# Experts of 64 in L2: slots of 32 rows in four column tiles instead of 64 rows in two, with sixteen weight homes

## The chip, the cores and the metric

The kernel runs on one core of a Trainium2 chip, in one launch. The metric is the device time of that launch in microseconds (us); lower is better. Before the change it is 2492.97 us, the median of three runs (2492.96 to 2495.43).

## The reference, cut to what matters

A chain of graph layers and mixture-of-experts layers over 625 nodes of 512 features. The change touches one of them, `L2_ffn`: each node picks 6 of 64 experts (a sigmoid router with a bias, first the best 4 of 8 groups of experts, then the best 6 in them), each picked expert computes a gated hidden layer of 160, and the six results are added with the node's weights. A shared expert of width 512 is added for all nodes.

```python
shared = jax.nn.silu(xf @ sWg) * (xf @ sWu) @ sWd
scores = jax.nn.sigmoid(xf @ router_w.T)
biased = scores + bias_corr
...
_, topk_idx = jax.lax.top_k(masked, 6)
w = jnp.take_along_axis(scores, topk_idx, axis=1)
w = w / (w.sum(axis=-1, keepdims=True) + 1e-20)
g = jnp.einsum('sc,ech->seh', xf, Wg)      # 512 -> 160, for each of 64 experts
u = jnp.einsum('sc,ech->seh', xf, Wu)
routed = jnp.einsum('seh,ehc->sc', combine[:, :, None] * jax.nn.silu(g) * u, Wd)
```

The kernel computes only the 3750 pairs of a node and a picked expert. A program that evaluates the reference on its inputs gives how they fall on the experts: 27 of the 64 get any rows, from 1 to 510 each, 3750 in all.

## The kernel before, in words

**Slots.** Rows of one expert are packed into slots of 64 rows; an expert with c rows takes ceil(c/64) slots. The worst case is 122 slots, so the program has 61 passes (`NU`) of two slots, one in each half of 128 rows. Every pass is in the program whether its slots have rows or not.

**Two blocks.** `l2_experts_block` (L2269) runs the router on DVE and the shared expert on PE side by side, then makes the tables: which expert owns each slot (`owner`, L2512), and which row sits in which place of which slot. The second table is built by 30 steps (L2524 to L2529): for each, DVE writes two one-hot operands (L2527 `place_hot`, L2529 `slot_value`), and PE multiplies them for each half (L2408), adding up in PSUM. PE then does the shared expert's `down` (L86 there). SyncE (SP) loads the first passes' weights (L2326 and on) and POOL gathers the first rows.

`l2_routed_blocks` (L2625) is the loop over passes. In iteration u of it, in this order, PE turns the rows of pass u+1 (`rows_transposed`, L2694), turns the hidden rows of pass u-1 (`hidden_transposed`, L2723; every fourth pass also the last 32 hidden columns of four passes at once, L2715), multiplies gate and up of pass u (`gate_up`, L2706: 4 k-tiles by 2 halves of 64 columns of the array, 320 columns streamed), multiplies the first 128 hidden columns of pass u-1 with Wd (`down`, L2731), and after every fourth pass the remaining 32 of four passes (`rest_down`, L2741). The two halves are column tiles of the array (`tile_position=(0, 64 * h)`): each has its own weights and rows. ACT copies the turned rows out (L2767) and computes silu (L2777). DVE multiplies (L2809, L2813), copies the turned hidden rows (L2790, L2796) and the result (L2803). POOL gathers rows eight passes ahead (L2557) and scatters results (L2563).

**Weights.** SP issues them by an order written out by hand. A pass u has for each half one main load (`Wgud`, 896 KB, L2597) and one rest load (64 KB, L2598). There are eight homes (`WR`) for mains, so pass u shares its homes with passes u-4, u-8 and so on; the slots are numbered so that such a chain holds neighbouring slots, mostly of one expert. A main is therefore fetched only when the expert changes within its home (`cond=new`), while a rest is fetched for every slot with rows (`cond=used`); a load that is left out is still issued, as an instruction that moves nothing. Expert numbers and conditions come from three tables, read eight entries at a time for four passes (L2591). The mains of pass u wait for `down(u-4)` (semaphore `d_mm`), which has read the same homes; rests wait for the `rest_down` two groups back (`y_mm`), as they have two buffers. The first two passes' weights are issued in the block ahead. At its start this block's SP also issues the next layer's weights (W1, W2 and three small ones, L2657 to L2661).

## Time and profile before

| | |
|---|---|
| median of 3 runs | 2492.97 us |
| the profiled execution | 2492.98 us, its span 2491.2 us |
| granted TensorE clock over the span | 0.964 of full |
| busy, share of the span | PE 94%, DVE 45%, ACT 29%, POOL 26% |
| moved by DMA | 281.58 MB, mean 113 GB/s |

The profile is of one execution. All windows are counted in us from the start of its span. The loop over passes runs from about 1834 to 2098 us, a tenth of the span. `PE` rows are matmuls, `PEld` rows are weight loads, `SPq` rows are instructions of SP's queue. An fp32 matmul of the program is two matmul instructions in the trace.

### The profile page before, as it was taken

How to read it: one execution, taken by the hardware profiler on the slowest of the kernel's cores; microseconds unless marked ns; L12 is line 12 of the kernel's file. 1: busy time of each engine (PE TensorE's matmuls, PEld its weight loads, DVE VectorE, ACT ScalarE, POOL GpSimd, SP SyncE). 2: the span in 40 equal slices, each digit the busy share in tenths (PEclk: the TensorE clock that was granted, in tenths of full speed). 3: DMA queues.
4: the chain of work that ended last, by engine and by line, in shares of the span. 5: the costliest groups of instructions: out<-in, count | busy, mean ns of one | idle time of the engine just before them, and what ended most of it. 6: DMA issues, size and time to landing. Idle time of an engine off the chain costs nothing. (4 is left out here: it accounts for less than half of the span.)

```text
span 2491.2 us, 33816 instructions
## 1 busy us (share of the span) xinstructions
PE 2335.4 (94%) x11401; PEld 1509.1 (61%) x11401; DVE 1126.0 (45%) x2712; ACT 717.6 (29%) x1398; POOL 649.4 (26%) x652
## 2 busy tenths in 40 slices
PE   5898969999999999999999999999989998889998
PEld 4475547757757765466576576576644444457775
DVE  8733985545545546735344344253623333530002
ACT  0422333323343322225134144153212221112211
POOL 0563666506506510000101101001124542101110
PEclk9898989999999998999999999999989998979999
DMA  3122026517507523020110110010056553558885
GB/s 90 49 72 72 1 84 213 147 31 232 150 28 228 152 69 112 17 81 1 58 60 22 37 60 23 34 51 13 18 174 230 176 187 116 123 201 306 319 292 194
DMA packets 73533, 281.58 MB, mean 113 GB/s; under 512 B 22298, under 2 KB 22426, under 8 KB 65438
## 3 DMA queue, kind: packets, MB, share of 16 engines
q1 hardware_dynamic: 38363, 188.09, 22.1%
q0 software_dynamic: 35008, 91.33, 12.4%
q8 instruction: 102, 1.67, 0.3%
q14 instruction: 60, 0.49, 0.1%
HBM read 354.71 MB, written 30.43 MB: 155 GB/s over the span
## 5 line engine op out<-in xcount | busy, mean ns | idle before, releaser
L86 PE MATMUL ps<-XT,W 128*128 128x250 f32 (+1 forms) x1200 | 334.6, 434 | 3.5 <-ACT XT L1420 1.6
L86 PEld LDWEIGHTS ps<-XT,W 128*128 128x128 f32 x1200 | 228.5, 193 | 106.1 <-issue 21.7
L1150 PE MATMUL ps<-XN,W 128*128 128x512 f32 x498 | 256.7, 598 | 2.6 <-ACT GT L1472 2.6
L1856 POOL TENSOR_TENSOR H<-H,RB 125x512 f32<-125x512 f32 x40 | 50.6, 1267 | 724.0 <-DVE XN L2179 611.6
L2706 PE MATMUL ps<-W,HT 128*64 128x320 f32 x976 | 146.2, 442 | 4.7 <-issue 4.7
L2563 POOL DMA_INDIRECT result_rows<-KT,LOGC x77 | 78.3, 1017 | 260.5 <-DVE KT L3292 212.7
L86 PE MATMUL ps<-W,HT 128*128 128x512 f32 (+1 forms) x312 | 139.9, 602 | 0.8 <-ACT HT L3261 0.5
L86 PEld LDWEIGHTS ps<-HT,W 128*128 128x128 f32 x1088 | 126.5, 195 | 8.8 <-issue 7.7
L86 PE MATMUL ps<-HT,W 128*128 128x128 f32 x1088 | 126.7, 278 | 0.8 <-DVE HT L3272 0.8
L1126 POOL DMA_INDIRECT XT<-node_rows,LOGC x81 | 77.1, 952 | 173.8 <-DMA node_rows<-V 122.3
L1288 PEld LDWEIGHTS ps<-P,QT 128*128 128x128 f32 x672 | 89.2, 194 | 44.4 <-issue 44.4
L1288 PEld LDWEIGHTS ps<-P,KT 128*128 128x128 f32 x672 | 88.1, 192 | 39.7 <-issue 39.7
L3261 ACT ACTIVATE HT<-ps,lcols 128x128 f32<-128x128 f32 x136 | 50.1, 368 | 211.3 <-PE ps L86 211.3
L1288 PEld LDWEIGHTS ps<-P,XT 128*128 128x128 f32 x648 | 85.2, 193 | 41.6 <-issue 41.4
L2232 DVE CUSTOM_DVE_ANT_0 P<-ps,LOGC 125x626 f32<-125x626 f32 x80 | 64.6, 807 | 96.0 <-PE ps L94 96.0
L86 PE MATMUL ps<-HT,V 125*128 125x125 f32 x800 | 102.7, 275 | 0.0
L2706 PEld LDWEIGHTS ps<-W,HT 128*64 128x64 f32 x976 | 65.4, 138 | 61.5 <-issue 16.1
L86 PEld LDWEIGHTS ps<-W,HT 128*128 128x128 f32 (+1 forms) x312 | 58.2, 191 | 71.7 <-issue 66.8
L94 PE MATMUL ps<-KT,QT 128*125 128x313 f32 x320 | 98.8, 430 | 0.0
L1126 POOL DMA_INDIRECT QT<-node_rows,LOGC x84 | 79.8, 950 | 65.4 <-PE ps L1288 42.7
L86 PEld LDWEIGHTS ps<-HT,V 125*128 125x128 f32 x800 | 95.7, 192 | 0.3
L1126 POOL DMA_INDIRECT KT<-node_rows,LOGC x84 | 79.4, 946 | 56.0 <-PE ps L1288 44.5
(618 smaller groups left out, 4175.4 us busy)
## 6 DMA issues: line engine op xcount, KB each, us to landing
W<-in_L_ffn_Wgud SPq DMA_DIRECT2D x122, 896.0 KB
W<-in_L_ffn_w SPq DMA_DIRECT2D x36, 2048.0 KB, 7.8
W<-in_L_gnn_Wqkv SPq DMA_DIRECT2D x4, 3072.0 KB, 9.9
W<-in_L_gnn_W SPq DMA_DIRECT2D x5, 2048.0 KB, 14.9
W<-in_L_gnn_Wm SPq DMA_DIRECT2D x4, 2048.0 KB, 7.7
W<-in_L_ffn_Wd_rest SPq DMA_DIRECT2D x122, 64.0 KB
W<-result_rows SPq DMA_DIRECT2D x5, 1344.0 KB
RB<-in_L_gnn_rows SPq DMA_DIRECT2D x24, 256.0 KB, 4.2
```

Source lines behind the costliest of these rows:

```text
L86: last = nc.tensor.matmul(out, lhs(k), rhs(k), start=(k == 0), stop=(k == nk - 1))
L94: last = nc.tensor.matmul(slot[0:m, a, 0:HF], lhs(k), rhs(k)[:, a * HF:(a + 1) * HF], start=(k == 0), stop=(k == nk - 1))
L1126: nc.gpsimd.indirect_dma_start(edges[n % GR], None, hb, bass.IndirectOffsetOnAxis(ap=b.slot_src[:, t:t + 1], axis=0)).then_inc(arrived[n % ...
L1150: nc.tensor.matmul(b.ps[:, n % PR, :], b.EAT[:, t * 128:(t + 1) * 128], We[layer], start=True, stop=True)\
L1288: last = nc.tensor.matmul(sums[:, k * 128:][:, bass.ds(off, R)], edges[n % GR][:, k * 128:(k + 1) * 128], hot[n % HR], start=False, stop=F ...
L1856: ins = nc.gpsimd.tensor_tensor(b.H[0:R, t, :], b.H[0:R, t, :], b.RB[0:R, at:at + D], ALU.add)
L2232: v.tensor_tensor_reduce(out=halves(P[i % 5]), in0=b.slot(0)[0:R, :, 0:HF], in1=halves(b.LOGC[0:R, t, :]), scale=1.0, scalar=-3e38, op0=AL ...
L2563: self.nc.gpsimd.indirect_dma_start(self.rows, bass.IndirectOffsetOnAxis(ap=self.b.slot_row[:, sl:sl + 1], axis=0), out, None, bounds_chec ...
L2706: last = nc.tensor.matmul(b.ps[HALF[h], 1 + u % 2, 0:2 * HE], xT[u % 2][:, k, HALF[h]], Wgu[(2 * u + h) % WR][:, k, :], start=(k == 0), st ...
L3261: nc.scalar.activation(hT[u][:, m, :], b.ps[:, 1 + m % 4, 0:128], ACT.Relu, bias=r.bias[u][:, m:m + 1]).then_inc(s["hidden_ready"], 1)
```

## The change

Slots have 32 rows, an expert with c rows takes ceil(c/32) of them, and a pass holds four, in the four column tiles of 32. The worst case is 180 slots, so there are 45 passes for 61. Four passes of four mains have sixteen homes, which lie in parts of eight tensors (`W`, `H`, `XN`, `V`, `P`, `XT`, `LOGC`, `HT`). Pass u still shares its homes with u-4. A rest load has one buffer for each home now, is fetched only when its main is (`step[4 + j]` conditions both), waits for the `rest_down` of the group before, and is issued two passes behind its main. There is one table, read for every pass (`read_step`). The next layer's W1 and W2 lie where homes are, so they are issued at the end of the loop. Rows are gathered six passes ahead for eight. In the block ahead the tables are 180 columns wide for 122, and the 30 steps multiply four quarters of 32.

The core of the diff (the index expressions of the tables that only change width are left out):

```diff
-    NE, NG, TG, K, NU, NH = r.ne, 8, 4, r.k, r.ns, 2 * r.ns
+    NE, NG, TG, K, NU, NH = r.ne, 8, 4, r.k, r.ns, 4 * r.ns
...
-            experts, news, useds = r.read_steps(sp, 0, 2 * r.early)
+            r.step_registers = [[sp.alloc_register(f"step{i}_{j}") for j in range(8)] for i in range(r.WR)]
             for u in range(r.early):
-                for h in range(2):
-                    r.load_weights(sp, u, h, experts[2 * u + h], news[2 * u + h], useds[2 * u + h])
+                step = r.read_step(sp, u)
+                for j in range(4):
+                    if u == 1 and j == 2:
+                        sp.wait_ge(s["up_mm"], len(units))
+                    r.load_main(sp, u, j, step)
...
-            for x in (*r.in_rows[0:4], vf[:, 375:384], vf[:, 634:2048]):
+            for x in (*r.in_rows[0:4], r.in_rows[5], vf[:, 2048:2560]):
...
-            pool.wait_ge(s["cleared"], 6)
+            nc.gpsimd.memset(r.in_rows[4], 0.0).then_inc(s["cleared"], 1)
+            pool.wait_ge(s["cleared"], 7)
...
-                for h in range(2):
-                    last = nc.tensor.matmul(b.ps[64 * h:64 * h + 64, 7, 0:NU], place_hot[j % RING],
+                for h in range(4):
+                    last = nc.tensor.matmul(b.ps[32 * h:32 * h + 32, 7, 0:NU], place_hot[j % RING],
                                             slot_value[j % RING][:, NU * h:NU * (h + 1)], start=(j == 0),
-                                            stop=(j == T * K - 1), tile_position=(0, 64 * h))
+                                            stop=(j == T * K - 1), tile_position=(0, 32 * h))
                 last.then_inc(s["table_mm"], 1)
...
-                v.tensor_scalar(place_hot[j % RING], b.iota[0:R, 0:64], in_slot[:, j:j + 1], None, ALU.is_equal)\
+                v.tensor_scalar(place_hot[j % RING], b.iota[0:R, 0:32], in_slot[:, j:j + 1], None, ALU.is_equal)\
...
-    WR, RR, GR, GU, early = 8, 2, 8, KD * 320, 2
-    CHAINS = WR // 2
+    WR, GR, GU, early = 4, 6, KD * 320, 2
 
     def __init__(self, nc, b, A, *args):
         super().__init__(nc, b, A, *args)
-        at = [1792 * ((u + 4) % self.WR) for u in range(self.WR)]
-        self.w_all = [b.W[:, x:x + 1792] for x in at]
-        self.w_gu = [b.W[:, x:x + self.GU] for x in at]
-        self.w_down = [b.W[:, x + self.GU:x + 1792] for x in at]
-        self.w_rest = [b.W[:, 14336 + 1024 * g:15360 + 1024 * g] for g in range(self.RR)]
-        self.steps = [b.LOGC[:, :, :].rearrange("p t n -> p (t n)")[:, at:at + 2 * self.ns].bitcast(I32)
-                      for at in (256, 896, 1024)]
-        self.in_rows = [*b.gathered, *(b.V[:, t, :] for t in range(4))]
-        self.gates = b.LOGC[:, :, :].rearrange("p t n -> p (t n)")[0:R, 576:576 + T * self.k]
-
-    def read_steps(self, sp, at, n):
-
-        kept = []
-        for i, table in enumerate(self.steps):
-            regs = [self.step_registers[i][j] for j in range(n)]
-            sp.load(regs, table[0:1, at:at + n])
-            kept.append([sp.snap(x, min_val=0, max_val=self.ne - 1 if i == 0 else 1) for x in regs])
-        return kept
-
-    def load_weights(self, sp, u, h, e, new, used):
-        home, q = (2 * u + h) % self.WR, 32 * (u % 4)
-        sp.dma_start(self.w_all[home], self.weights("L2_ffn_Wgud", e), cond=new).then_inc(self.w_in[home], 16)
-        sp.dma_start(self.w_rest[u // 4 % self.RR][q:q + 32, 512 * h:512 * (h + 1)], self.weights("L2_ffn_Wd_rest", e),
-                     cond=used).then_inc(self.rest_in[u // 4 % self.RR], 16)
+        xn, hf, vf = (x[:, :, :].rearrange("p t n -> p (t n)") for x in (b.XN, b.H, b.V))
+        xt, ht = (x[:, :, :].rearrange("p k n -> p (k n)") for x in (b.XT, b.HT))
+        pf, lf = (x[:, :, :].rearrange("p t n -> p (t n)") for x in (b.P, b.LOGC))
+        homes = [(b.W, 7168), (b.W, 8960), (b.W, 10752), (b.W, 12544),
+                 (hf, 0), (b.W, 14336), (b.W, 0), (b.W, 1792),
+                 (xn, 0), (vf, 0), (pf, 0), (b.W, 3584),
+                 (xt, 0), (lf, 1024), (ht, 2880), (b.W, 5376)]
+        self.w_all = [x[:, at:at + 1792] for x, at in homes]
+        self.w_gu = [x[:, at:at + self.GU] for x, at in homes]
+        self.w_down = [x[:, at + self.GU:at + 1792] for x, at in homes]
+        self.w_rest = [x[:, at:at + 512] for x, at in ((pf, 2048), (pf, 2560), (xt, 1792), (vf, 2048))]
+        self.steps = lf[:, 640:640 + 8 * self.ns].bitcast(I32)
+        self.in_rows = [*b.gathered, xn[:, 1792:2304], hf[:, 2048:2560]]
+        self.gates = lf[0:R, 576:576 + T * self.k]
+
+    def read_step(self, sp, u):
+
+        regs = self.step_registers[u % 4]
+        sp.load(regs, self.steps[0:1, 8 * u:8 * u + 8])
+        return [sp.snap(x, min_val=0, max_val=self.ne - 1 if i < 4 else 1) for i, x in enumerate(regs)]
+
+    def load_main(self, sp, u, j, step):
+        home = 4 * (u % self.WR) + j
+        sp.dma_start(self.w_all[home], self.weights("L2_ffn_Wgud", step[j]), cond=step[4 + j])\
+            .then_inc(self.w_in[u % self.WR], 16)
+
+    def load_rest(self, sp, u, j, step):
+        q = 32 * (u % 4)
+        sp.dma_start(self.w_rest[j][q:q + 32, :], self.weights("L2_ffn_Wd_rest", step[j]), cond=step[4 + j])\
+            .then_inc(self.rest_in[u // 4 % 2], 16)
...
+            steps = [r.read_step(sp, u) for u in range(WR)]
+            for u in range(r.early, WR):
+                for j in range(4):
+                    r.load_main(sp, u, j, steps[u])
+            for u in range(2):
+                for j in range(4):
+                    r.load_rest(sp, u, j, steps[u])
+            clear_retired(sp, retired)
+            for u in range(WR, NU + 2):
+                if u < NU:
+                    steps.append(r.read_step(sp, u))
+                    sp.wait_ge(s["d_mm"], u - WR + 1)
+                    for j in range(4):
+                        r.load_main(sp, u, j, steps[u])
+                if u - 2 >= 4:
+                    sp.wait_ge(s["y_mm"], 4 * ((u - 2) // 4))
+                for j in range(4):
+                    r.load_rest(sp, u - 2, j, steps[u - 2])
+            sp.wait_ge(s["d_mm"], NU - 3)
             sp.dma_start(W1[:, :], A["L3_gnn_W12"][:, 0:2048]).then_inc(p.g3_weights, 16)
+            sp.wait_ge(s["d_mm"], NU - 1)
             sp.dma_start(W2[:, :], A["L3_gnn_W12"][:, 2048:4096]).then_inc(p.g3_weights, 16)
             sp.dma_start(b.RB[:, 0:1024], A["L3_gnn_b12"].partition_broadcast(128)).then_inc(p.g3_rows, 16)
             sp.dma_start(b.router[:, 0:KD * 8], A["L3_ffn_gate_w"]).then_inc(p.f3_in, 16)
             sp.dma_start(b.RB[:, 1856:1864], A["L3_ffn_gate_b"].partition_broadcast(128)).then_inc(p.f3_in, 16)
-            clear_retired(sp, retired)
-            for u in range(r.early, NU):
-                j = 2 * (u - r.early) % 8
-                if j == 0:
-                    experts, news, useds = r.read_steps(sp, 2 * u, min(8, 2 * (NU - u)))
-                if 2 * u >= WR:
-                    sp.wait_ge(s["d_mm"], u - WR // 2 + 1)
-                if u >= 4 * RR:
-                    sp.wait_ge(s["y_mm"], 4 * (u // 4 - RR + 1))
-                for h in range(2):
-                    r.load_weights(sp, u, h, experts[j + h], news[j + h], useds[j + h])
...
-                for h in range(2):
-                    pe.wait_ge(w_in[(2 * u + h) % WR], 16 * ((2 * u + h) // WR + 1))
+                pe.wait_ge(w_in[u % WR], 64 * (u // WR + 1))
                 if u >= 2:
                     pe.wait_ge(s["h_ready"], 2 * (u - 1))
                 for k in range(KD):
-                    for h in range(2):
-                        last = nc.tensor.matmul(b.ps[HALF[h], 1 + u % 2, 0:2 * HE], xT[u % 2][:, k, HALF[h]],
-                                                Wgu[(2 * u + h) % WR][:, k, :], start=(k == 0), stop=(k == KD - 1),
-                                                tile_position=(0, 64 * h))
+                    for j in range(4):
+                        last = nc.tensor.matmul(b.ps[QUARTER[j], 1 + u % 2, 0:2 * HE], xT[u % 2][:, k, QUARTER[j]],
+                                                Wgu[4 * (u % WR) + j][:, k, :], start=(k == 0), stop=(k == KD - 1),
+                                                tile_position=(0, 32 * j))
...
-                for h in range(2):
-                    last = nc.tensor.matmul(b.ps[HALF[h], 4 + u % 4, :], hT[u % 4][:, HALF[h]],
-                                            r.w_down[(2 * u + h) % WR], start=True, stop=False, tile_position=(0, 64 * h))
+                for j in range(4):
+                    last = nc.tensor.matmul(b.ps[QUARTER[j], 4 + u % 4, :], hT[u % 4][:, QUARTER[j]],
+                                            r.w_down[4 * (u % WR) + j], start=True, stop=False, tile_position=(0, 32 * j))
...
-                pe.wait_ge(r.rest_in[g % RR], 32 * sum(members(i) for i in range(g % RR, g + 1, RR)))
+                pe.wait_ge(r.rest_in[g % 2], 64 * sum(members(i) for i in range(g % 2, g + 1, 2)))
                 for q in range(members(g)):
                     group = slice(32 * q, 32 * q + 32)
-                    for h in range(2):
-                        last = nc.tensor.matmul(b.ps[HALF[h], 4 + q, :], restT[g % 2][group, HALF[h]],
-                                                r.w_rest[g % RR][group, 512 * h:512 * (h + 1)], start=False, stop=True,
-                                                tile_position=(32 * q, 64 * h))
+                    for j in range(4):
+                        last = nc.tensor.matmul(b.ps[QUARTER[j], 4 + q, :], restT[g % 2][group, QUARTER[j]],
+                                                r.w_rest[j][group, :], start=False, stop=True,
+                                                tile_position=(32 * q, 32 * j))
...
-    for i, (ne, k, ns, size) in enumerate(((64, 6, 61, 64), (8, 2, 17, 128))):
+    for i, (ne, k, ns, size) in enumerate(((64, 6, 45, 32), (8, 2, 17, 128))):
```

How the order moves on PE, in one iteration that ends a group of four passes (a row is: line of the program, operation, output and inputs, columns of the array by columns streamed, how many in a row; `HT` holds the turned rows, the other name is the home of the weights). Before:

```order
L2694 MATMUL ps<-ident,V 128x128 x4
L2723 MATMUL ps<-ident,HT 128x128
L2715 MATMUL ps<-ident,HT 128x128
L2706 MATMUL ps<-W,HT 64x320 x8
L2731 MATMUL ps<-W,HT 64x512 x2
L2741 MATMUL ps<-W,HT 64x512 x8
```

With the change, in the same place:

```order
L2712 MATMUL ps<-ident,H 128x128 x4
L2740 MATMUL ps<-ident,HT 128x128
L2732 MATMUL ps<-ident,HT 128x128
L2723 MATMUL ps<-W,HT 32x320 x16
L2748 MATMUL ps<-XT,HT 32x512
L2748 MATMUL ps<-LOGC,HT 32x512
L2748 MATMUL ps<-HT 32x512
L2748 MATMUL ps<-W,HT 32x512
L2758 MATMUL ps<-P,HT 32x512 x2
L2758 MATMUL ps<-XT,HT 32x512
L2758 MATMUL ps<-V,HT 32x512
```

The sequence of steps in an iteration stays; each has twice the matmuls, half as wide, and the same columns streamed. (The last three rows repeat four times, for four passes.)

On SP, what is issued for one pass in the middle of the loop. Before, after a read of the tables (three loads from `LOGC` for four passes), where an `ISA` works out an address and the `DMA` behind it is the load, whether it moves anything or not:

```order
L2591 TENSOR_LOAD LOGC
L2592 ISA
L2597 ISA
L2597 DMA W<-in_L_ffn_Wgud 128x1792
L2598 ISA
L2598 DMA W<-in_L_ffn_Wd_rest 32x512
L2597 ISA
L2597 DMA W<-in_L_ffn_Wgud 128x1792
L2598 ISA
L2598 DMA W<-in_L_ffn_Wd_rest 32x512
```

With the change, for every pass (two of the four rests of two passes ago are shown):

```order
L2597 TENSOR_LOAD LOGC
L2598 ISA
L2602 ISA
L2602 DMA XN<-in_L_ffn_Wgud 128x1792
L2602 ISA
L2602 DMA V<-in_L_ffn_Wgud 128x1792
L2602 ISA
L2602 DMA P<-in_L_ffn_Wgud 128x1792
L2602 ISA
L2602 DMA W<-in_L_ffn_Wgud 128x1792
L2607 ISA
L2607 DMA P<-in_L_ffn_Wd_rest 32x512
```

So a pass takes eight loads and one read of the table for four loads and three quarters of a read.

## Rows read from the trace of the kernel before

**Rows 1.** Windows: length; busy of PE, PEld, DVE, ACT, POOL; clock, DMA share, GB/s.

```profile
1834.00:1850.00 16.00, 10.23 (x62) 5.44 (x64) 1.35 (x6) 3.00 (x6) 4.03 (x4) 0.92 0.93 327
...
1950.00:2000.00 50.00, 50.00 (x357) 23.65 (x353) 15.86 (x51) 10.82 (x24) 24.88 (x25) 1.00 0.55 174
```

**Rows 2.** Timeline of PE over one group's end and one pass.

```profile
1956.81 2.38 PE L2706 MATMUL ps<-W,HT 128*64 128x320 f32 x16
1959.01 1.03 PE L2731 MATMUL ps<-W,HT 128*64 128x512 f32 x4
1959.97 1.11 PE L2741 MATMUL ps<-W,HT 32*64 32x512 f32 x16
...
1961.71 2.38 PE L2706 MATMUL ps<-W,HT 128*64 128x320 f32 x16
...
1965.57 1.57 PE L2706 MATMUL ps<-W,HT 128*64 128x320 f32 x10
```

**Rows 3.** Chain that ended last: the first and the last full rest_down of 15.

```profile
1860.52 1.04 PE ps L2741 x16
...
2092.33 1.04 PE ps L2741 x16
```

**Rows 4.** Line L2706 alone: duration ns min/median/max, first and last start.

```profile
L2706 PEld LDWEIGHTS ps<-W,HT x976: 132/137/230, 1836.1 to 2090.8; 128*64 128x64 f32 x196
L2706 PE MATMUL ps<-W,HT x976: 432/432/792, 1836.1 to 2091.0; 128*64 128x320 f32 x196
```

**Rows 5.** Timeline, the weight loads of a rest_down.

```profile
2092.26 0.23 PEld L2741 LDWEIGHTS ps<-W,HT 32*64 32x64 f32 x16 [0.81 <-issue]
```

**Rows 6.** DMA queue and kind in 1834 to 2098 us, then in 1790 to 1834: packets, MB.

```profile
q1 hardware_dynamic: 8352, 33.97, 38.4%
...
q1 hardware_dynamic: 576, 2.95, 15.8%
```

**Rows 7.** Timeline of SP's queue: start, duration of the issue.

```profile
1842.15 0.08 SPq L2597 DMA_DIRECT2D W<-in_L_ffn_Wgud  x1
1842.52 0.08 SPq L2598 DMA_DIRECT2D W<-in_L_ffn_Wd_rest  x1
1842.88 0.35 SPq L2597 DMA_DIRECT2D W<-in_L_ffn_Wgud  x1
1843.51 0.77 SPq L2598 DMA_DIRECT2D W<-in_L_ffn_Wd_rest  x1
...
1854.28 0.08 SPq L2598 DMA_DIRECT2D W<-in_L_ffn_Wd_rest  x1
1856.92 0.07 SPq L2597 DMA_DIRECT2D W<-in_L_ffn_Wgud  x1
```

**Rows 8.** An issue, and the DMA share in 1865 to 1873 us (slices of 0.2 us).

```profile
1865.70 0.36 SPq L2597 DMA_DIRECT2D W<-in_L_ffn_Wgud  x1
DMA  0432585299416797989979899976588520007664
```

**Rows 9.** Timeline of PE at the third pass.

```profile
1843.16 0.27 PE L2723 MATMUL ps<-ident,HT 128*128 128x128 f32 x1
...
1848.10 3.74 PE ps L2706 x16
...
1853.39 2.30 PE ps L2706 x16
```

**Rows 10.** Timeline of DVE in the 30 steps of the table.

```profile
1806.77 0.24 DVE L2527 TENSOR_SCALAR LOGC<-iota,P 125x64 f32<-125x64 f32 x1
1806.93 0.33 DVE L2529 TENSOR_SCALAR LOGC<-LOGC,P 125x122 f32<-125x122 f32 x1
1807.18 0.24 DVE L2527 TENSOR_SCALAR LOGC<-iota,P 125x64 f32<-125x64 f32 x1
```

**Rows 11.** Timeline at the end of the loop.

```profile
2096.08 1.43 PE L2741 MATMUL ps<-W,HT 32*64 32x512 f32 x4
...
2098.41 0.69 DVE L2803 TENSOR_SCALAR KT<-ps 128x512 f32<-128x512 f32 x1 [1.69 <-DMA result_rows<-KT,LOGC]
```

More of the change, by code:

```diff
@@ L2277, in l2_experts_block @@
     r.w_in = p.sems(*(f"f2_w_in{u}" for u in range(r.WR)))
-    r.rest_in = p.sems(*(f"f2_rest_in{u}" for u in range(r.RR)))
+    r.rest_in = p.sems(*(f"f2_rest_in{u}" for u in range(2)))
     r.arrived = p.sems(*(f"f2_rows_in{u}" for u in range(r.GR)))
@@ L2304, in l2_experts_block, with by_quarter, in_steps @@
     diag, behind = lf[0:NE, 1216:1216 + NE], lf[0:NE, 1280:1280 + NH]
-    place_hot = [lf[0:R, 1408 + 64 * i:1472 + 64 * i] for i in range(RING)]
-    slot_value = [lf[0:R, 1792 + 128 * i:1792 + 128 * i + NH] for i in range(RING)]
-    order, order_int = lf[:, 2560:2560 + NH], lf[:, 2752:2752 + NH].bitcast(I32)
-    row_float = lf[:, 2912:2912 + NU]
-    owner, has_rows = lf[:, 640:640 + NH], lf[:, 768:768 + NH]
-    is_new, changed = ht[:, 4480:4480 + NH], ht[:, 4608:4608 + 2 * (NU - r.CHAINS)]
-    def by_half(x):
-        return x.rearrange("p (h u) -> p h u", h=2)
-    def in_steps(x):
-        return x.rearrange("p (u h) -> p h u", h=2)
+    place_hot = [lf[0:R, 1472 + 32 * i:1504 + 32 * i] for i in range(RING)]
+    slot_value = [lf[0:R, 1664 + 192 * i:1664 + 192 * i + NH] for i in range(RING)]
+    order, order_int = lf[:, 2816:2816 + NH], ht[:, 4480:4480 + NH].bitcast(I32)
+    row_float = lf[:, 3000:3000 + NU]
+    owner = ht[:, 4660:4660 + NH]
+    clipped, has_rows, is_new = (pf[:, at:at + NH] for at in (1920, 2240, 2560))
+    changed = ht[:, 4840:4840 + 4 * (NU - r.WR)]
+    def by_quarter(x):
+        return x.rearrange("p (j u) -> p j u", j=4)
+    def in_steps(i):
+        return r.steps.rearrange("p (u i j) -> p i j u", i=2, j=4)[:, i, :, :]
     tops, idx, idxf = b.top_val, b.top_idx, b.top_idxf
@@ L2326, in _ @@
             sp.wait_ge(s["used"], 1)
-            r.step_registers = [[sp.alloc_register(f"step{i}_{j}") for j in range(8)] for i in range(3)]
-            experts, news, useds = r.read_steps(sp, 0, 2 * r.early)
+            r.step_registers = [[sp.alloc_register(f"step{i}_{j}") for j in range(8)] for i in range(r.WR)]
             for u in range(r.early):
-                for h in range(2):
-                    r.load_weights(sp, u, h, experts[2 * u + h], news[2 * u + h], useds[2 * u + h])
+                step = r.read_step(sp, u)
[3 more added lines that the diff above has]
+                    r.load_main(sp, u, j, step)
             sp.wait_ge(s["row"], 1)
@@ L2490, in _ @@
             dve.wait_ge(s["counted"], 1)
-            c.link(v.tensor_scalar(slots, b.ps[0:NE, 4, 0:1], 63.0, None, ALU.add))
+            c.link(v.tensor_scalar(slots, b.ps[0:NE, 4, 0:1], 31.0, None, ALU.add))
             c.link(v.tensor_copy(slots_int, slots))
-            c.link(v.tensor_scalar(slots_sh, slots_int, 6, None, ALU.arith_shift_right))
+            c.link(v.tensor_scalar(slots_sh, slots_int, 5, None, ALU.arith_shift_right))
             v.tensor_copy(slots, slots_sh).then_inc(s["slots"], 1)
             dve.wait_ge(s["slots"], 1)
-            dve.wait_ge(s["order"], 4)
+            dve.wait_ge(s["order"], 8)
             c.mark(v.tensor_copy(order, order_int))
@@ L2499, in _ @@
             c.link(v.tensor_copy(first, b.ps[0:NE, 4, 2:3]))
-            v.tensor_scalar(diag, b.ident[0:NE, 0:NE], first, 64.0, ALU.mult, ALU.mult).then_inc(s["first"], 1)
+            v.tensor_scalar(diag, b.ident[0:NE, 0:NE], first, 32.0, ALU.mult, ALU.mult).then_inc(s["first"], 1)
             c.link(v.tensor_tensor(ends, first, slots, ALU.add))
@@ L2629, in l2_routed_blocks @@
     HE, HM = 160, 128
-    NU, WR, RR, GR, YR, LAG = r.ns, r.WR, r.RR, r.GR, 4, 6
+    NU, WR, GR, YR, LAG = r.ns, r.WR, r.GR, 4, 6
     W1 = b.H[:, :, :].rearrange("p t n -> p (t n)")[:, 0:2048]
@@ L2645, in l2_routed_blocks @@
     restT = [ht[:, 2624 + 128 * i:2752 + 128 * i] for i in range(2)]
-    HALF = (slice(0, 64), slice(64, 128))
+    QUARTER = [slice(32 * j, 32 * j + 32) for j in range(4)]
     def members(g):
@@ L2799, in _ @@
                     q = u - 5
-                    dve.wait_ge(s["y_mm"], 4 * (q // 4) + members(q // 4))
+                    dve.wait_ge(s["y_mm"], q + 1)
                     if q >= YR:
```

28 lines of the change are left out of this document (14 added, 14 removed).

## The prediction

> **What bounds the kernel now.** The page first: PE is busy for 94% of the span, so look where it is busy with little. Then the windows around the loop over passes: from the fourth pass on PE is busy all the time at full clock, while DMA engines stand half idle [rows 1]. So the loop costs what PE's steps cost. The timeline shows one iteration: 16 gate and up matmuls 2.38 us, four of `down` 1.03, turned rows in between, and in every fourth `rest_down` 1.11, each overlapping the next a little [rows 2]. From gate to gate it is 3.86 us without `rest_down` (1961.71 to 1965.57) and 4.90 with it (1956.81 to 1961.71). Over the loop: the chain has 14 groups from 1860.52 to 2092.33 [rows 3], 16.56 us each, **4.14 us a pass**. Last, line L2706 alone: a matmul of 320 columns takes 432 ns by itself, but 16 of them take 2.30 in the chain, 0.29 for a pair. The two column tiles stream side by side, and weight loads of 137 ns [rows 4] are hidden under them.
>
> **Loads.** Numbering the slots by the order in the code, with the reference's rows per expert, I get for before 75 slots in use and 32 main loads, and for the change 132 slots in use and 39 main loads. The trace confirms the first: 33.97 + 2.95 MB by the hardware queue [rows 6] are 32 mains (0.917 MB each, 29.4), 75 rests (4.9) and the next layer's 2.6. By pass, the change loads 3, 3, 3, 3, then one or none, but two in passes 13, 18, 36 and 44. Rests are now 39 as well.
>
> **The change part by part.** All against the profiled execution's 2492.98 us, which is the median to 0.01.
>
> 1. *Sixteen passes go*: 16 x 4.14 = **-66.2**. This takes four tiles to cost what two cost. Each of 45 passes streams the same columns per tile. No row of before has four column tiles over all 128 rows, so the price lies between nothing (as for the second tile) and twice the time of each step (pairs in turn). I take nothing, since `rest_down` is nearest: it has eight tiles in flight (4 row groups by 2 halves), 16 matmuls in 1.11 us [rows 2]. Issue is no limit: 16 weight loads of 0.13 start within 0.23 us [rows 5], 7 ns apart. Two more tiles start 13 ns later in each step: 45 x 0.03 = **+1.3**.
> 2. *The tables*: DVE paces the 30 steps, 0.162 us from L2527 to L2529 and 0.255 on to the next [rows 10]. That is 1.6 ns per column (58 columns between them, 0.093 us). 32 columns fewer and 58 more: +0.04 a step, 1.3, and eight wider table operations 0.2: **+1.5**. PE's doubled matmuls there (16 instructions with their weight loads per 0.46 us) stay under it at 7 ns an issue. The `memset` in POOL's chain and two gathers fewer are off the path, which is PE's `down` up to the block's end.
> 3. *The start of the loop*. Six early mains (5.5 MB, 17 us at 327 GB/s [rows 1]) are issued from 1801 on and are there before 1834. Passes 2 and 3 bring three mains each, ahead of them only four table reads. An issue that moves nothing costs SP 0.36 us, a main 0.63, a rest 0.6 to 1.05 [rows 7]; three table reads and an address are 2.64, so a read is 0.76. First main 3.2 us into the block, 2.75 MB at 327 GB/s, 1 us before and 1 behind: pass 2's weights are there at 13.7. Before, its gate began at 14.1 (1848.10), held by W1 and W2, which now go last. Pass 3 needs 8.4 more, 22.1, and began at 19.3 (1853.39) [rows 9]: +2.8. The wait leaves the clock halved for a pass, as in 3.74 for 2.30 [rows 9]: +1.4. The first group's rests queue behind: +0.8. **+5**.
> 4. *SP in steady state*. A pass now costs SP 0.76 + 8 x 0.36 = 3.7, and 0.5 more for each pair that moves: 4.2 with one, against PE's 4.14. Once in four passes its wait for `y_mm` holds it for `rest_down` (1.04), then four rests (1.7) and a read (0.76) follow, before the next pass's mains: 3.5 late, and it hardly ever catches up. Mains of u are released by `down(u-4)`, 2 x 3.86 + 0.7 = 8.4 us before gate u. That leaves 4.9. A load issued at 1865.70 keeps the engines busy until about 1871 [rows 8], so one load takes about 5 and just fits: **+1.5** for all of them. A second takes 0.917 MB / 327 GB/s = 2.8 more and waits 2.3: in 18, 36 and 44, **+6.9**.
> 5. *Rests*. The rests of 11 are issued behind the two mains of 13: 3.5 + 1 + 5.6 + 1.3 = 11.4 us after `down(9)`, where `rest_down` wants them after 8.3: +3.1. Those of 23, behind one main: +0.9. **+4**.
> 6. *The end*. Pass 44's rests may be issued only after `rest_down(10)`, near 2093.4 in before's time, take 1.7 to issue and some 2.3 to land: 2097.4 for 2096.08. The last copy waited until 2098.41 anyway [rows 11], so +0.4. W1, W2 and the small ones (2.6 MB, 8 us of transfer) now run beside the last scatters: 0 to 3, I take 1.6. PE needs them only some 20 us later. **+2**.
>
> Sum: -66.2 + 1.3 + 1.5 + 5 + 1.5 + 6.9 + 4 + 2 = -44.0. **2492.98 - 44.0 = 2449.0 us.** ACT, DVE and POOL do the same per pass as before, and their cover (a pass of 4.14) keeps its length.
>
> **A rule against it.** The row first: the weight loads of L2706 (976, 137 ns each) lie under streaming matmuls that share all 128 rows with them [rows 4]. The Trainium skill ("TensorE: Matmul & The Clock Gate", Part 3, what overlaps and what doesn't) says that a weight load overlaps matmuls in flight only when its row group differs. This case's trace speaks against it for two tiles; for four no row does, so it is a rival.
>
> **Rivals.**
>
> - *No waits for weights* (loads land in 4, or SP is quicker): terms 1 to 3 alone, **2434**. For it: before, after its third pass, PE never waited. Against it: twice the issues, with the same lead. Chance 0.15.
> - *SP becomes the bound.* If issues are as slow as the 1.05 of one rest in rows 7 for every second load, and every pass costs it 4.6, then 41 passes are 0.45 longer, +18, in place of some of 4 and 5: **2462**, at most 2480. Against it: most of its issues move nothing. Chance 0.18.
> - *Four tiles run as two pairs*, the other side: gate 2.30 more, `down` 0.86, `rest_down` 1.04 in four, +3.42 a pass, 154 in 45, the waits under it gone: 2493 - 66 + 154 + 6 = **2587**. It decides as soon as four tiles take 1.5 us a pass more than two, 1.4 times as long. For it: each tile reads its own stream, and no row shows four per partition. Against it: two cost nothing extra, and nor do eight in `rest_down`. Chance 0.06.
> - *Weight loads come out from under the streams.* One per round of four tiles at 137 ns [rows 4], 10.5 rounds a pass: 1.44 x 45 = 65, the waits of 4 and 5 gone: 2449 + 65 - 12 = **2502**, slower. Chance 0.03. This is what the Trainium skill's rule above would make of it; by it the sum would be 2502.
> - *That it doesn't do what it says* could only be in the loads, since 45 passes are in the program. With 39 mains for 32 I have counted them; 10 more would cost 2.8 each at worst, within the range. For a time within 0.2% of before I leave 0.01.
>
> **How the numbers follow.** My forecast has the rest, 0.57, and spans 2438 to 2460. Adding most of the first two rivals gives **2430 to 2472**, which leaves out the slower ones (0.09), the tail of SP's and a little below. About 0.2% (5 us) is what a measurement of this kernel can tell from no change. Faster 0.15 + 0.18 + 0.57 = 0.90, same 0.01, slower 0.09.
>
> **What would show it.** Gate matmuls of 32 x 320: 32 in 2.3 to 2.4 us, and 3.9 from gate to gate where nothing waits. The loop ends some 45 us earlier. PE waits ahead of the gates of passes 2 and 3 (about 4 each), 18, 36 and 44 (about 2), and ahead of `rest_down(2)` (about 3), and SP's queue is never idle for long. Mains that are in the trace number 39. I am wrong if gates take over 3 us (tiles or weight loads), if waits are spread over all passes (SP), or if there are none after pass 3.

## The result and the profile after

The changed kernel takes 2471.92 us (median of 4, 2471.29 to 2475.01), where the kernel before took 2494.11 beside it: ratio 0.9913, 95% interval 0.9901 to 0.9925. It is faster by 22 us. The forecast was 44 faster, a time of 2449.0; the result lies at the upper end of the range, 2472.

The page's head, a line of its busy times and one of its groups:

```profile
span 2469.6 us, 35201 instructions
PE 2282.7 (92%) x12133; PEld 1474.8 (60%) x12133; DVE 1105.7 (45%) x2643; ACT 703.2 (28%) x1366; POOL 615.8 (25%) x625
DMA packets 70260, 285.73 MB, mean 116 GB/s; under 512 B 19274, under 2 KB 19402, under 8 KB 62158
L2723 PE MATMUL ps<-W,HT 128*32 128x320 f32 x824 | 116.5, 473 | 9.6 <-issue 9.6
```

A pass first, against [rows 2]. The timeline of PE, a gate whose four tiles all read W, and `down` two passes on; then the duration of that line's instructions, against [rows 4]:

```profile
2003.49 2.36 PE L2723 MATMUL ps<-W,HT 128*32 128x320 f32 x32
...
2010.60 1.04 PE L2748 MATMUL ps<-W,HT 128*32 128x512 f32 x8
```

```profile
L2723 PEld LDWEIGHTS ps<-W,HT x824: 106/110/178, 1839.8 to 2067.8; 128*32 128x32 f32 x165
L2723 PE MATMUL ps<-W,HT x824: 429/433/743, 1839.8 to 2068.0; 128*32 128x320 f32 x165
```

Twice the matmuls in the same 2.36 and 1.04 us: four column tiles cost what two did. The windows are against [rows 1] (length; busy of PE, PEld, DVE, ACT, POOL; clock, DMA share, GB/s):

```profile
1834.00:1850.00 16.00, 12.18 (x96) 5.36 (x94) 2.04 (x7) 3.00 (x6) 4.03 (x4) 0.89 0.56 214
1850.00:1870.00 20.00, 15.12 (x131) 6.36 (x131) 1.60 (x8) 2.11 (x5) 2.01 (x2) 0.74 0.94 281
1900.00:1920.00 20.00, 13.96 (x156) 6.19 (x152) 4.01 (x13) 2.49 (x6) 5.85 (x7) 0.85 0.60 218
1950.00:2000.00 50.00, 46.38 (x602) 20.68 (x605) 14.96 (x49) 10.21 (x23) 22.57 (x22) 1.00 0.61 201
1995.00:2015.00 20.00, 20.00 (x262) 8.98 (x258) 6.18 (x19) 4.51 (x10) 9.90 (x10) 1.00 0.34 114
```

Only 1995 to 2015, where no load moves for six passes, looks as the loop did before. Elsewhere PE stands still, at gates ("issue": the profile names no releaser, the gate waits for its weights) and at `rest_down`:

```profile
1851.31 0.43 PE L2723 MATMUL ps<-XN,HT 128*32 128x320 f32 x1 [2.98 <-issue]
1860.49 0.71 PE L2723 MATMUL ps<-XT,HT 128*32 128x320 f32 x1 [3.57 <-issue]
1882.93 0.52 PE L2723 MATMUL ps<-XT,HT 128*32 128x320 f32 x1 [2.31 <-issue]
...
1914.55 1.06 PE L2758 MATMUL ps<-P,HT 32*32 32x512 f32 x2 [5.29 <-DMA V<-in_L_ffn_Wd_rest]
1942.14 0.43 PE L2723 MATMUL ps<-XN,HT 128*32 128x320 f32 x1 [2.46 <-issue]
...
2025.88 1.83 PE L2723 MATMUL ps<-W,HT 128*32 128x320 f32 x12 [5.24 <-issue]
...
2064.83 3.36 PE L2723 MATMUL ps<-W,HT 128*32 128x320 f32 x28 [4.16 <-issue]
```

These are the gates of passes 2, 3 and 7, `rest_down(2)`, and the gates of 18, 36 and 44. The last gates also show a half clock: 28 matmuls in 3.36 us.

**Where the time went.** Call the time from the start of gate u-1 to the start of gate u step u. Every undisturbed step is 3.84, 3.84, 3.95 or 4.93 us, 16.56 in four passes, as before to 0.03. What a step takes beyond that is its excess, and so the loop can be added up (us, from the starts of the gates in the two traces; the 44 undisturbed steps make 180.7, the 60 of before 246.9):

```
                                       after   less before   forecast
to the first gate (1839.80, 1836.05)             +3.7        +1.5  term 2
undisturbed steps, 180.7 for 246.9              -66.2       -64.9  term 1
excess of steps 1 to 4, 11.9 for 5.8             +6.1        +5    term 3
excess of steps 5 to 44, 32.4 for 0.3           +32.1       +12.4  terms 4, 5
  one load:  steps 7, 8, 11, 12, 27, 35   7.9                 1.5
  two loads: steps 18, 36, 37, 44        14.0                 6.9
  rests:     steps 5, 13, 14, 25         10.2                 4
last gate to the end, 404.7 for 402.1            +2.6        +2    term 6
sum                                             -21.6       -44.0
```

So the gain came in full, and 32 us of it were given back in the steady part of the loop, 20 more than forecast. The sum is steady, the single step is not: in two kernels below whose loop is the same (those that only move layer 3's loads) steps 5 to 44 have 35.4 and 34.4 of excess, but pass 7 doesn't wait in the first, and in the second pass 23 does. Nor is the split by cause sharp in step 13: behind `rest_down(2)`'s wait lies a gate whose own second main was 2.5 late as well (it landed at 1913.4 for a gate due at 1911.0).

### The profile page after: what moved, and what is told of

It reads as the page before. It is cut to its first block and busy times, and to the rows that moved or that the text cites. A ratio compares the mean times of both kernels' runs of the same rounds, so it can differ in the third digit from the quotient of the medians.

```text
span 2469.6 us, 35201 instructions
## 1 busy us (share of the span) xinstructions
PE 2282.7 (92%) x12133; PEld 1474.8 (60%) x12133; DVE 1105.7 (45%) x2643; ACT 703.2 (28%) x1366; POOL 615.8 (25%) x625
## 2 busy tenths in 40 slices
DMA packets 70260, 285.73 MB, mean 116 GB/s; under 512 B 19274, under 2 KB 19402, under 8 KB 62158
## 5 line engine op out<-in xcount | busy, mean ns | idle before, releaser
L2567 POOL DMA_INDIRECT result_rows<-KT,LOGC x61 | 62.0, 1016 | 257.9 <-DVE KT L3309 211.6
L2723 PE MATMUL ps<-W,HT 128*32 128x320 f32 x824 | 116.5, 473 | 9.6 <-issue 9.6
L2083 ACT ACTIVATE P<-P,nmax 125x626 f32<-125x626 f32 x80 | 65.4, 818 | 98.9 <-DVE nmax L2237 98.8
```

Source lines behind the costliest of these rows:

```text
L2083: nc.scalar.activation(P[j % 5], P[j % 5], ACT.Exp, bias=b.nmax[0:R, j:j + 1], accum_out=b.den[0:R, j:j + 1]).then_inc(s["exp"], 1)
L2567: self.nc.gpsimd.indirect_dma_start(self.rows, bass.IndirectOffsetOnAxis(ap=self.b.slot_row[:, sl:sl + 1], axis=0), out, None, bounds_chec ...
L2723: last = nc.tensor.matmul(b.ps[QUARTER[j], 1 + u % 2, 0:2 * HE], xT[u % 2][:, k, QUARTER[j]], Wgu[4 * (u % WR) + j][:, k, :], start=(k == ...
```

## Experiments

Two theories for those 32 us. **SP's order**: SP issues all loads from one queue, stands at `y_mm` once in four passes and issues mains late ever after. **The data**: 39 mains and 39 rests (2048-byte packets) take longer than the lead of four homes, whenever they are issued.

### The rests one pass later

```diff
-            for u in range(2):
-                for j in range(4):
-                    r.load_rest(sp, u, j, steps[u])
+            for j in range(4):
+                r.load_rest(sp, 0, j, steps[0])
...
-            for u in range(WR, NU + 2):
+            for u in range(WR, NU + 3):
...
-                if u - 2 >= 4:
-                    sp.wait_ge(s["y_mm"], 4 * ((u - 2) // 4))
+                if u - 3 >= 4:
+                    sp.wait_ge(s["y_mm"], 4 * ((u - 3) // 4))
                 for j in range(4):
-                    r.load_rest(sp, u - 2, j, steps[u - 2])
+                    r.load_rest(sp, u - 3, j, steps[u - 3])
```

> The rests of pass u - 3, not of pass u - 2, behind the four main loads of pass u. SP's wait for the rests' buffer then asks for a rest_down that follows directly on the down which the mains of the same pass have just waited for, where it now asks for one that comes a pass later. SP-order theory (the waits in the loop come from SP standing 2.7 to 3.4 us late): mains of passes 7, 11, 18, 27, 36 and 44 go out 1.5 to 2.5 us sooner, single waits of 2.6 shrink to under 1, those of 18, 36 and 44 by 2 each, and with them some half-clock passes: 8 to 15 us less than the changed kernel, 2457 to 2464. Data theory (the transfers themselves are too much for the lead of four passes): the same transfers take as long, at most 3 us less, 2469 to 2472. Against both: rests go out one issue later, so a rest_down may wait more.

2465.53 us, ratio 0.9884 (0.9868 to 0.9901), 6 less than the changed kernel: between what the two theories gave. The trace says why. How long after the start of gate u-3 the first main of pass u was issued, mean over passes 8 to 44 by u mod 4 (`down(u-4)`, which releases it, ends some 3.2 behind that start):

```
u mod 4                              0     1     2     3
changed kernel                      6.2   6.0   5.7   8.2
rests one pass later                3.8   3.9   3.9   4.0
no rests (below)                    3.5   3.5   3.5   3.5
all issued, nothing moves (below)   5.7   5.5   5.3   7.0
another order (below)               4.4   6.1   4.7   3.6
```

With the rests one pass later SP is on time, and the gates of 7, 11, 27, 36 and 44 no longer wait. But the rests that end a group are now too late, at `rest_down(2)`, (5) and (8), 5.5 to 6.2 us of excess each:

```profile
1907.92 1.06 PE L2757 MATMUL ps<-P,HT 32*32 32x512 f32 x2 [4.09 <-DMA V<-in_L_ffn_Wd_rest]
```

One wait took the other's place: the excess of steps 5 to 44 is 30.2.

### Without rests, and without any data

In the first, the rests of passes 4 to 44 are not loaded (`if u - 2 < 4` ahead of their loop, no wait for `y_mm`, and `rest_down` waits for the first four passes' rests).

> The rests of passes 4 to 44 are left out, their issues, their bytes and SP's wait for their buffer; rest_down uses the rests of the first four passes. SP-order theory: from pass 7 on no gate waits but perhaps those with two loads (18, 36, 44) under 1 us each, no rest_down waits (2 and 5 had 5.9 + 1.0 and 1.8), and few passes at half clock: 25 to 30 us less than the changed kernel, 2442 to 2447. Data theory: 32 mains from pass 4 on still have to come with 3 to 4 us of slack less than they want, about 10 us less, 2460 to 2464, the two rest_down waits among it.

In the second nothing is new from pass 4 on:

```diff
-                                   ALU.not_equal))
+                                   ALU.is_lt))
```

> From pass 4 on no expert counts as new, so every main and rest load is still issued by SP but none of them moves data; the passes compute with the weights of passes 0 to 3. This prices the instructions alone: by the forecast 4.14 a pass, of 44 steps 182 us for 225 to 228, less the waits of passes 2 and 3 and the slow steps around them (some 11 us), which stay: 33 to 36 us less than the changed kernel, 2436 to 2439. If PE or SP itself were the bound (SP issues 8 loads, a read and the waits in every pass), the steps would stay above 4.14 and the time above 2445.

2435.81 and 2439.57 us, one run each. Both lie outside their ranges, the first 6 below the order theory's 2442, the second 0.6 above. Of the first's 36 us the loop has 28.4; 5.5 lie behind its last gate (399.3 us for 404.7) and 1.6 ahead of its first, which no theory spoke of. So the excess is the better measure. That of steps 5 to 44 is 5.2 and 0.2. The second's steady part, then the first's:

```profile
1950.00:2000.00 50.00, 50.00 (x647) 21.91 (x643) 16.16 (x53) 10.80 (x24) 24.83 (x25) 1.00 0.26 87
```

```profile
1950.00:2000.00 50.00, 50.00 (x647) 21.91 (x643) 15.88 (x51) 10.84 (x25) 24.97 (x25) 1.00 0.58 201
```

With every issue in place and no byte moved, PE never waits: SP's issues by themselves don't bound the loop. But they do make SP late: by the table the order alone, with nothing moving, holds the mains back by 1.8 to 3.5 more than without rests. With the mains' bytes and no rests 3.6 are lost, in steps 13, 18 and 36; of the rest of the 5.2 a wait of 1.2 for the first four passes' rests, which are still loaded, is nearly all. The other 27 come with the rests, by their issues or their bytes.

### The same bytes in another order

```diff
-            for u in range(WR, NU + 2):
+            for u in range(WR, NU + 3):
...
-                if u - 2 >= 4:
-                    sp.wait_ge(s["y_mm"], 4 * ((u - 2) // 4))
-                for j in range(4):
-                    r.load_rest(sp, u - 2, j, steps[u - 2])
+                late = {3: (u - 3, u - 2), 0: (u - 2, u - 1)}.get(u % 4, ())
+                for q in late:
+                    if q < NU:
+                        if q >= 4:
+                            sp.wait_ge(s["y_mm"], 4 * (q // 4))
+                        for j in range(4):
+                            r.load_rest(sp, q, j, steps[q])
```

> Only SP's order moves: the rests of passes 4g and 4g+1 go out behind the mains of pass 4g+3, those of 4g+2 and 4g+3 behind the mains of 4g+4, none in the two steps after. SP waits for rest_down(g-1) where it directly follows the down that it has just waited for, and every rest is out before its rest_down by more than a pass. SP-order theory (the bytes are the same, what costs is when they are issued): nearly all of what leaving the rests out gave (28 us of the loop) comes here too, less one or two two-load passes that still wait 1 to 3: 18 to 26 us less than the changed kernel, 2446 to 2454. Data theory (the rests' own bytes, in 2048-byte packets, slow the mains): as with the rests merely one pass later, 2462 to 2466. Passes 2 and 3 wait as before in both.

**2445.78 us, ratio 0.9809 (0.9796 to 0.9823)**: 26 us less than the changed kernel, with the same loads (285.73 MB in both traces). The excess of steps 5 to 44 is 5.5, as without rests. This settles it: SP's order was worth 27 us, and the rests' bytes cost nothing that can be told when they go out in this order. One thing is not taken apart: the order changes both how late the mains go out and which loads run beside each other. Pass 36, by the two timelines of SP's queue, that of the changed kernel first:

```profile
2012.14 0.43 SPq L2607 DMA_DIRECT2D P<-in_L_ffn_Wd_rest  x2
...
2014.96 1.70 SPq L2602 DMA_DIRECT2D W<-in_L_ffn_Wgud  x4
```

```profile
1991.54 0.43 SPq L2607 DMA_DIRECT2D P<-in_L_ffn_Wd_rest  x2
1992.24 0.07 SPq L2607 DMA_DIRECT2D XT<-in_L_ffn_Wd_rest  x1
1992.60 0.07 SPq L2607 DMA_DIRECT2D V<-in_L_ffn_Wd_rest  x1
1993.71 1.70 SPq L2602 DMA_DIRECT2D W<-in_L_ffn_Wgud  x4
```

The gates of pass 33 began at 2008.4 and 1989.8: the mains of pass 36 went out 6.6 and 3.9 us behind. The second of them landed at 2025.3 for a gate that was due at 2020.6, and at 2001.4 for one due at 2001.5.

### The start

> Three homes of pass 2 (the first 1792 columns of XN, V from column 768 and XT) are filled in the block ahead, behind those of passes 0 and 1, while the queue stood idle from 1821 to 1840; the rest buffer in V moves to its first columns. If the waits ahead of passes 2 and 3 (3.3 and 3.9 us) and their half clock (2.7 and 3.8 for 2.3, the step behind pass 3 2.7 too long) are a loss of their own: all go, with part of the 1.3 ahead of rest_down(0): 9 to 13 us less than the changed kernel, 2459 to 2463. If they only hide later ones (the mains of passes 4 to 7 would land no sooner, and pass 7 wait longer): 3 to 4 us less, 2468.

```diff
-                 (xn, 0), (vf, 0), (pf, 0), (b.W, 3584),
-                 (xt, 0), (lf, 1024), (ht, 2880), (b.W, 5376)]
+                 (xn, 0), (vf, 768), (xt, 0), (b.W, 3584),
+                 (pf, 0), (lf, 1024), (ht, 2880), (b.W, 5376)]
...
+            step = r.read_step(sp, r.early)
+            for j in range(3):
+                r.load_main(sp, r.early, j, step)
             sp.wait_ge(s["row"], 1)
...
```

2468.54 us, ratio 0.9901 (0.9885 to 0.9918), which can't be told from the changed kernel. The time is the second case's, its mechanism is not: pass 7 waits less than in the changed kernel and steps 5 to 44 have the same excess (32.2), so nothing was shifted into them. The loop is 6 us shorter, but from the last gate to the end it takes 408.4 us for 404.7, and why is open. In the trace pass 2 no longer waits, and steps 1 to 4 have 6.1 of excess for 11.9. Pass 3 waits longer:

```profile
1853.45 0.43 PE L2727 MATMUL ps<-P,HT 128*32 128x320 f32 x1 [4.71 <-issue]
```

Its third main, issued at 1840.2, landed at 1851.0, beside six rests of passes 0 and 1. The next moves these behind:

> The order of the rests and the early homes of pass 2 together, with the rests of pass 1 behind the mains of pass 4 and those of 2 and 3 behind those of pass 5, so that the third main of pass 3 (which landed at 1851.0 beside six rests) has fewer beside it. If the two losses are separate, the gains add: 18 to 26 for the order and 8 to 11 for the start (the early loads alone gave 6 in the loop, with pass 3 still waiting 5.0): 2436 to 2446. If the start only shifts waits to later passes, 2446 to 2450.

```diff
+                if u < 6:
+                    late = (1,) if u == 4 else (2, 3)
```

**2438.13 us, ratio 0.9778 (0.9765 to 0.9792)**, the fastest of all and 34 less than the changed kernel. Steps 1 to 4 have 3.8 of excess, but 5 to 44 have 9.4 (5.5 in the kernel without the start): part of the gain moved on, to `rest_down(0)` (1.6, in step 5) and step 28 (1.7 for 0.5).

### The end

> The two loads of 1 MB for layer 3 wait until the scatter of pass 40 has landed; nothing else moves. In the changed kernel that scatter went out at 2072.73 beside them and the copy of the last result waited for it until 2080.59, 6.84 us; the kernel before had 1.69 there. If the two loads are what delays it, the copy comes 4 to 5 us sooner and the whole time is 3 to 5 us less, 2467 to 2469. Rival: layer 3 then waits for its weights, or the scatter is slow by itself: no difference, 2471 to 2473.

```diff
+            sp.wait_ge(scattered[(NU - 1) % YR], 16 * ((NU - 1) // YR))
             sp.wait_ge(s["d_mm"], NU - 3)
```

2475.11 us, ratio 0.9929 (0.9915 to 0.9943): no gain. In its trace the loop, which is the same, takes 3.0 us more, so the time alone says little. What was expected ahead did come, in the timeline of DVE; first the changed kernel, then this one:

```profile
2080.59 0.69 DVE L2820 TENSOR_SCALAR KT<-ps 128x512 f32<-128x512 f32 x1 [6.84 <-DMA result_rows<-KT,LOGC]
```

```profile
2078.11 0.69 DVE L2821 TENSOR_SCALAR KT<-ps 128x512 f32<-128x512 f32 x1 [1.65 <-DMA result_rows<-KT,LOGC]
```

But the 2.5 MB now stood between the scatters and the 7.7 MB of rows that layer 3 reads back, and its sums over these rows waited longer for them (the groups of 2085 to 2200 us, the changed kernel's first):

```profile
L3085 DVE SCALAR_TENSOR_TENSOR X<-W,LOGC,X 125x512 f32<-125x512 f32 x30 | 26.1, 870 | 2.2 <-DMA W<-result_rows 1.3
```

```profile
L3086 DVE SCALAR_TENSOR_TENSOR X<-W,LOGC,X 125x512 f32<-125x512 f32 x30 | 26.2, 875 | 7.5 <-DMA W<-result_rows 6.6
```

So the loads were put behind these rows:

> The end of the changed kernel alone: W1 (1 MB) is loaded behind the first tile of rows that layer 3 reads back, its bias rows (0.5 MB) behind the second and W2 (1 MB) behind the fifth, where the changed kernel has all three ahead of the rows and beside the last scatters. W1's first use comes some 2 us after the first tile's normalisation, W2's some 50 us later. If those 2.5 MB stand on the path (beside the scatter, or ahead of the rows, as the run that only delayed them suggests), both goes: the copy of the last result 4 to 5 us sooner and the rows no later, 5 to 8 us less than the changed kernel, 2464 to 2467. Rival: W1 is now waited for behind the first tile, and what is gained ahead is given back: 2470 to 2473.

```diff
+                if t == 0:
+                    sp.dma_start(b.H[:, :, :].rearrange("p t n -> p (t n)")[:, 0:2048], A["L3_gnn_W12"][:, 0:2048])\
+                        .then_inc(p.g3_weights, 16)
+                if t == 1:
+                    sp.dma_start(b.RB[:, 0:1024], A["L3_gnn_b12"].partition_broadcast(128)).then_inc(p.g3_rows, 16)
...
+                .then_inc(p.g3_second, 16)
```

2470.73 us, ratio 0.9916 (0.9898 to 0.9933): the rival's time, no difference. PE's turned tiles of layer 3, the first, second and last of five, in the changed kernel and in this one:

```profile
2101.39 1.07 PE L2937 MATMUL ps<-ident,XN 125*128 125x125 f32 x4 [8.67 <-DVE XN L3077]
2110.84 0.65 PE L2937 MATMUL ps<-ident,XN 125*128 125x125 f32 x4 [1.51 <-DVE XN L3077]
...
2133.95 0.65 PE L2937 MATMUL ps<-ident,XN 125*128 125x125 f32 x4 [1.51 <-DVE XN L3077]
```

```profile
2097.60 1.07 PE L2939 MATMUL ps<-ident,XN 125*128 125x125 f32 x4 [8.80 <-DVE XN L3080]
2109.87 1.10 PE L2939 MATMUL ps<-ident,XN 125*128 125x125 f32 x4 [3.52 <-DVE XN L3080]
...
2134.55 0.65 PE L2939 MATMUL ps<-ident,XN 125*128 125x125 f32 x4 [1.51 <-DVE XN L3080]
```

Counted from the last gate (2064.83 and 2064.80), the first tile is 3.8 us earlier, the second 0.9, the last 0.6 later. So the gain was given back between the first tile and the last. It was not by a wait for W1, as the rival had it: PE waits for DVE's normalised tiles in both, the second of them 2.0 longer, with W1 now loaded ahead of that tile's rows. Three kernels more had an end of this kind on top of the fastest:

> As the one before, with the end changed too: the rests of pass 44 go unconditionally to buffers of their own (in RB and GT) and so wait for no rest_down, and layer 3's two loads wait for the scatter of pass 40. Where rest_down waited 1.5 us for them and the copy of the last result 6.8 us: 5 to 7 us less than the kernel of the run before this one, 2430 to 2440. Rival: nothing, since layer 3 is bound by its own loads.

> Order of the rests, early homes of pass 2 and this end together. The three places don't overlap, so the gains add: 5 to 8 us less than the run with the first two (2438.1), 2430 to 2433. If W1 is waited for: 2436 to 2440.

> As the run before, with the rests of pass 44 in buffers of their own, loaded without a wait for rest_down. The 1.4 us ahead of the last rest_down goes: 1 to 1.5 us less than the run before. Rival: no difference, because the last copy waits for the scatter of pass 40 and not for rest_down.

The first and the third load pass 44's rests with no wait for `rest_down` (four buffers in RB and GT, their `dma_start` without the condition); the first has W1 and W2 behind the scatter of pass 40 too, the second and third have them behind the rows. 2442.06, 2442.96 and 2441.56 us, ratios 0.9794 (0.9781 to 0.9807), 0.9792 (0.9779 to 0.9804) and 0.9798 (0.9786 to 0.9811): none better than 0.9778, and all three intervals overlap its interval. The first two missed their ranges. The third's median is the foretold 1.4 below the second's, but that can't be told from nothing: its ratio is the higher of the two. From the last gate to the end the nine of these kernels that load all rests have 405.0 to 408.4 us, the changed kernel 404.7, whatever the order there. The spread of 3.4 is wider than most of what was looked for.

### What a wait costs beyond its length

```diff
+                for _ in range({14: 8, 22: 14, 30: 20, 38: 26}.get(u, 0)):
+                    v.tensor_scalar(b.RB[:, 512:1024], b.RB[:, 0:512], 1.0, None, ALU.mult).then_inc(s["hold"], 1)
```

> What a wait of PE costs beyond its length. The kernel in which nothing moves from pass 4 on (every step 3.84, 3.84, 3.95 or 4.93) with DVE held at passes 14, 22, 30 and 38 by 8, 14, 20 and 26 useless copies of 128x512, so that PE stands still by some 1, 3, 6 and 8 us with nothing else on its path changed. If the lost time behind the waits of the changed kernel (gates of 2.7 to 3.8 us for 2.3) is PE's clock falling while it stands: the granted clock falls behind the longer holds and the steps behind them are 1 to 4 us too long in sum, the shorter hold costs only its own length. If it was the transfers that slowed the matmuls (they ran beside them then, and none does here): all gates 2.2 to 2.3, and the steps too long by the holds alone.

2469.42 us, one run. PE stood 1.3, 4.2, 7.0 and 9.3 us (start to start, less the 0.49 of the four transposes ahead), and the loop lost 1.7, 7.0, 8.8 and 11.2: 0.4, 2.8, 1.8 and 1.9 more than the stand. The windows before, in and behind the second hold:

```profile
1945.00:1949.00 4.00, 4.00 (x49) 1.73 (x45) 3.06 (x9) 0.90 (x2) 2.21 (x3) 1.00 0.31 105
1949.00:1954.00 5.00, 0.75 (x8) 0.42 (x4) 4.66 (x12) 0.60 (x1) 1.20 (x2) 0.83 0.28 98
1954.00:1958.00 4.00, 3.78 (x29) 1.54 (x33) 1.05 (x4) 0.00 (x0) 1.03 (x1) 0.50 0.00 0
```

Behind it the granted clock is 0.50, 1.2 GHz, while the DMA engines move nothing. So it is the clock, not the transfers, that makes the matmuls behind a wait slow. The changed kernel shows the same: behind `rest_down(2)`'s wait, in 1914 to 1920, its granted clock is 0.50 with the DMA engines at 6%. Here waits of 4 to 9 us cost 1.8 to 2.8 more.

## Why the prediction was off

1. **Term 1 was right** (-66.2, measured the same; the 1.3 for the starts of tiles did not appear). Four column tiles go at the price of two; the rival of two pairs (2587) fell with the first gate at full clock. So did the rival of the weight loads (2502): the gate has 32 of them at 110 ns, 3.5 us, inside 2.36 us. The Trainium skill ("TensorE: Matmul & The Clock Gate", Part 3, what overlaps and what doesn't) lets a weight load overlap matmuls in flight only when its row group differs; all these share all 128 rows, and the trace does not agree.
2. **Term 2** (+1.5): +3.7 in this pair of traces, of which its mechanism is the smaller part. The 30 steps took 12.9 us for 12.5, +0.4 for the foretold 1.3. The rest is the clock and the start. The shared expert's `down` behind them took 20.2 us for 18.6, as the granted clock was 0.50 until 1821.7 (before: until 1816.8); of the thirteen kernels with the change ten have 20.0 to 20.3 there and three 18.6, and before has one trace, so how much of it is the change's stays open. Turned tiles at half clock ahead of the first gate are 0.4 more. The remaining 1.4 is that the steps began later, which varies among these kernels from 1800.2 to 1803.7. In those with the same code up to there the first gate began at 1837.7 to 1840.5.
3. **Term 3** (+5): 6.1. Pass 2 waited 3.0 and pass 3 3.6, about 4 each as foretold, and the slow clock stayed into step 4, 2.7 too long.
4. **Term 4 failed** (+8.4, measured 21.9). Its first half holds: SP was some 3.5 late at the group's end (4.1 on average, without pass 15, which stood behind the wait of `rest_down(2)`) and hardly caught up: in the other three passes it was 2.3 to 2.9 behind on average. What failed is "one load takes about 5 and just fits: +1.5". From pass 7 on the first main that a pass moves took 5.45 us on average from its issue to its last packet, and 4.3 to 7.1 singly, for 4.85 in the kernel with the rests moved. That the longest ones come of rests or the next pass's main beside them is likely, but no run shows it by itself. The forecast left no slack, and a load that is estimated to just fit can miss as well: 7.9 us. For a second load it said 2.3 to wait, where its own 5 + 2.8 against 4.9 make 2.9; the second loads took 7.7 to 9.3 and cost 2.5, 7.3 (with the step behind) and 4.2.
5. **Term 5 failed** (+4, measured 10.2). `rest_down(2)` waited 5.3 for the foretold 3.1, then the step behind it lost 1.4. `rest_down(5)` had 1.2 for 0.9.
6. **In both no half clock was priced**, though term 3 had it. Behind the waits at gate 7, `rest_down(2)` and gate 36 the clock is halved, and steps 8, 14 and 37 are 1.7, 1.4 and 2.0 too long by it, step 13 is by 1.5: 6.6 of the 32 us, which are counted in the terms above. Gate 44 adds 1.3 in the next term. It doesn't come with every wait: at gates 18 and 27 PE waited 2.5 and 2.3 us and lost nothing more, at gate 7 it waited 2.3 and lost 1.7.
7. **Term 6** (+2): 2.6, right by luck. The last copy waited 6.84 for 1.69 [rows 11] and began 15.8 us behind the last gate for 9.3, 6.5 more, where the forecast had at most 2. From there to layer 3's first tile it took 20.8 us for 22.9, and from that to the end 1.7 less than before. Neither was foretold, and no run shows why.

The rival "SP becomes the bound" (2462) named the right engine with the wrong mechanism. The kernel in which all is issued and nothing moves has no lost step, and the one with another order moves every byte and loses 5.5: SP's rate was enough and its order was not. That rival had set the range's upper end, so the result lies inside the range by luck. Of the list of signs, gates in 2.3 to 2.4 us, 39 mains, waits at 2, 3, 18, 36, 44 and `rest_down(2)` came true; those at 7, 11 and 27 and the end only 24 us sooner (last gate 2064.8 for 2089.1) were the wrong part.

## What to carry to other kernels

When one queue issues loads for two consumers, write down for each issue when it may go and when it is due, and put the wait that comes last behind everything that doesn't need it; here 27 us hung on a few lines, and merely moving the wait by one pass gave the loss to the other consumer. Count every pass whose slack is under a microsecond as a miss in a forecast, with its length, and where it stands for more than 4 us with 1.3 to 3 us of half clock on top. Ahead of any work on the end of a stage, add up what the DMA engines must move there: here reordering loads that all had to pass before the same point gave nothing, twice.

## What was not expected of the hardware

Weight loads were shorter with half the columns (110 ns for 32, 137 for 64), and 32 matmuls of four tiles took the 2.36 us of 16 of two, with no loss at all. A hold of 4.2 us cost more in half clock (2.8) than holds of 7.0 and 9.3 (1.8 and 1.9): the granted clock was already coming back sooner behind the long ones (0.61 and 0.57 in the four microseconds behind them, 0.50 behind the short one). In the trace it had fallen 1.9 us before PE went on at the hold of 4.2, and 3.9 and 7.2 before at the long ones, and was full again 4.9, 2.9 and 3.0 behind: more of the slow stretch fell into the stand. In the first loads of the loop the DMA engines were busy all the time at two thirds of the 327 GB/s of [rows 1], with rests in 2048-byte packets beside a main:

```profile
1856.00:1861.00 5.00, 1.43 (x14) 0.76 (x13) 0.29 (x1) 0.60 (x1) 1.00 (x1) 0.82 1.08 212
```
